# Four pieces of an fp4 weight rounding moved from the front into the layers, and all weight transposes into the last stage

## The reference, cut to what matters

```python
# 1. token part: patches -> 9 windows per token, local attention over them, then one global class token
q = ln(red) @ la_wq;  k, v = ln(win) @ la_wkv;  agg = softmax(q*scale @ k) @ v
local = red + agg @ la_proj_w + la_proj_b
cls_out = cls + attention(ln(cls) @ ga_wq, ln(local) @ ga_wkv) @ ga_proj_w + ga_proj_b
h = concat([local @ mod_w + mod_b, cls_out])
# 2. two layers of delta-rule attention and a gated feed-forward part, on layernorm(h)
h = h + attn(layernorm(h))
# 3. feed-forward part whose activations and weights are rounded to fp4 in blocks of 16
def fp4_quant_dequant(x):
    scale = max(max(abs(xb)) / 6, 1e-12)                  # one per 16 values
    return GRID[searchsorted(MID, abs(xb / scale))] * sign(xb) * scale
h = h + fp4_linear(silu(fp4_linear(y, w_gate)) * fp4_linear(y, w_up), w_down)   # y = layernorm(h)
```

## Time and profile before

| | us |
|---|---|
| median of 3 runs | 394.76 |
| lowest and highest | 392.4, 395.17 |
| profiled execution | 392.98 |
| its span | 391.2 |

### The profile page before, as it was taken

The page is one execution under the profiler, slowest core; times in us unless marked ns, Lnnn a source line. Parts: engine busy times, 40 slices in busy tenths (PEclk is TensorE's granted clock), DMA queues, the critical chain, the costliest instruction groups (busy, mean ns, idle before and its releaser), DMA issues.

```text
span 391.2 us, 9485 instructions
## 1 busy us (share of the span) xinstructions
PE 309.1 (79%) x4346; PEld 228.1 (58%) x4346; DVE 204.0 (52%) x359; ACT 88.7 (23%) x187; POOL 43.9 (11%) x33
## 2 busy tenths in 40 slices
PE   0999449968992478698388999897488999868966
PEld 0556346757981356465387857565487857555443
DVE  3029987995469436214755222114755221159993
ACT  1132002301211013455012122255012122231020
POOL 0744951200032000000000000000000000000000
PEclk9999958998998559899688699999588599989989
DMA  8999910000000000000000030230000000000001
GB/s 187 333 330 215 339 61 0 3 0 0 1 2 0 0 0 2 1 0 2 2 2 3 2 109 2 59 169 2 3 0 3 2 3 0 1 0 0 2 0 34
DMA packets 2521, 18.26 MB, mean 47 GB/s; under 512 B 441, under 2 KB 761, under 8 KB 1729
## 3 DMA queue, kind: packets, MB, share of 16 engines
q1 hardware_dynamic: 2497, 17.91, 15.0%
HBM read 17.58 MB, written 0.33 MB: 46 GB/s over the span
## 4 chain that ended last, share of the span: by engine, by line
PE 47%; DVE 31%; DMA 10%; ACT 5%; issue 3%; POOL 3%; SPq 1%; DVEq 0%; ACTq 0%
DMA big<-in_patches 10%; PE ps L1229 10%; PE ps L1074 5%; PE ps L1225 4%; PE ps L1014 4%; PE ps L1378 3%; PE ps L1293 3%; PE ps L1341 2%; DVE big L891 2%; PE ps L1024 2%; DVE big L919 2%; DVE qa L572 2%; PE ps L1302 2%; DVE wt L916 2%; DVE big L901 2%
## 5 line engine op out<-in xcount | busy, mean ns | idle before, releaser
L1024 PE MATMUL ps<-big,cwb 120*128 120x384 f32 x120 | 42.8, 515 | 10.4 <-DMA big<-in_patches 10.4
L1024 PEld LDWEIGHTS ps<-big,cwb 120*128 120x128 f32 x120 | 24.1, 204 | 26.7 <-issue 13.5
L1074 PE MATMUL ps<-wkvg,pecT 128*128 128x256 f32 x144 | 33.7, 395 | 4.8 <-ACT big L360 4.8
L1225 PE MATMUL ps<-cst,ones 128*128 128x320 f32 x112 | 36.5, 476 | 0.0
L1074 PEld LDWEIGHTS ps<-wkvg,pecT 128*128 128x128 f32 x144 | 28.2, 198 | 9.1 <-DVE prod L687 3.7
L1229 PE MATMUL ps<-cwb,wl 128*128 128x320 f32 x120 | 33.3, 435 | 0.0
L1225 PEld LDWEIGHTS ps<-cst,ones 128*128 128x128 f32 x112 | 23.4, 214 | 9.9 <-issue 2.6
L1229 PEld LDWEIGHTS ps<-cwb,wl 128*128 128x128 f32 x120 | 22.5, 190 | 10.6 <-issue 0.9
L1293 PE MATMUL ps<-wt,big 32*32 32x32 f32 x1280 | 16.6, 213 | 13.0 <-DVE wt L894 10.6
L262 POOL TENSOR_TENSOR xs<-xs,big 120x640 f32<-120x640 f32 x14 | 22.8, 1629 | 8.6 <-DMA big<-in_patches 7.8
L1293 PEld LDWEIGHTS ps<-wt,big 32*32 32x32 f32 x1280 | 14.9, 125 | 15.1 <-DVE wt L894 11.5
(11 more groups left out here) (224 smaller groups left out, 485.8 us busy)
## 6 DMA issues: line engine op xcount, KB each, us to landing
big<-in_patches SPq DMA_DIRECT2D x6, 900.0 KB, 26.2
wl<-in_layers SPq DMA_DIRECT2D x2, 2176.0 KB, 26.8
wt<-in_tok SPq DMA_DIRECT2D x1, 2304.0 KB, 17.7
wf<-in_ffn SPq DMA_DIRECT2D x1, 2112.0 KB, 26.4
wl<-in_layers SPq DMA_DIRECT2D x2, 1040.0 KB, 23.2
cwb<-in_conv SPq DMA_DIRECT2D x1, 600.0 KB, 5.1
out<-h SPq DMA_DIRECT2D x5, 64.0 KB, 2.0
cst<-in_constants SPq DMA_DIRECT2D x1, 304.0 KB, 39.4
```

The lines of the kernel that those rows point to most:

```text
L1024: last = mm(ps[:, i % 4, 0:GRP], cwc[:, k, c * P:(c + 1) * P], xg[:, g, k, :], start=(k == 0), stop=(k == KC - 1))
L1074: last = mm(ps[:, 2 * w + un % 2, t * C:(t + 1) * C], pecT[:, c, i * P:(i + 1) * P], wkvg[:, c, w * C:(w + 1) * C], start=(c == 0), stop=( ...
L1225: mm(ps[:, bank, 0:NT], ones[:, :], cst[:, 0:NT], start=True, stop=True)
```

## The change

Pieces 0 and 1 of the rounding stay in the front. Piece 2 + 2l goes to the head of layer l, behind `normed`; piece 3 + 2l to its end, one part ahead of each addition into x and the last part behind them. All nine groups of transposes go to the last stage, behind the transposes of x, into banks 6 and 7, and all weight copies on ScalarE behind its last table load. The twelve clock-holding products there become four, behind the weight transposes. `sf` moves from `wf` to columns 3200 to 7040 of `big`, and GpSimd's zeroing of a part of `act` waits for the scores of the global attention in place of the last transposes.

```diff
--- before.py
+++ after.py
@@ -132,7 +132,7 @@
         rkq = pf[:, 2560:3840].rearrange("p (a j n) -> p a j n", a=2, j=CH)
         bt = pf[:, 3840:4480].rearrange("p (j n) -> p j n", j=CH)
 
-        sf = wf[:, :]
+        sf = big[:, 3200:7040]
         kh = sf[:, 0:640].rearrange("p (j n) -> p j n", j=CH)
         kbq = sf[:, 640:1920].rearrange("p (a j n) -> p a j n", a=2, j=CH)
         act = sf[:, 1920:3840].rearrange("p (i n) -> p i n", i=FC)
@@ -280,7 +280,7 @@
             w1 = sc[:, 1, :, HD:H].unsqueeze(3).broadcast_to([P, NP_, H - HD, DH])
             nc.gpsimd.tensor_tensor(v1, v1, w1, ALU.mult).then_inc(S["vprod"], 1)
 
-            pool.wait_ge(S["wq_t"], 9)
+            pool.wait_ge(S["ga_s"], 1)
             nc.gpsimd.memset(act[0:64, FC - 1, :], 0.0).then_inc(S["zeros"], 1)
             for l in range(LAYERS):
 
@@ -365,7 +365,7 @@
 
                 for i in range(first, end):
                     act_.wait_ge(S["wq_t"], i + 1)
-                    b = 4 + i % 2
+                    b = 6 + i % 2
                     if i < 6:
                         nt = min(4, 11 * 2 - 4 * i)
                         dst = wguT[:, :, :].rearrange("p c (i n) -> p i c n", i=11)[:, 2 * i:2 * i + nt // 2]
@@ -408,11 +408,9 @@
             rsqrt(act_, rsg, ps[:, 1, 0:NW], "ga_rs", EPS_LN, k=1)
             act_.wait_ge(S["ga_max"], 2)
             nc.scalar.activation(ge[:, :, :, :], ge[:, :, :, :], ACT.Exp, scale=SCALE).then_inc(S["ga_e"], 1)
-            weights_out(0, 6)
 
             act_.wait_ge(S["x_c"], 1)
             nc.scalar.activation(sqx[:, :, :], xT[:, :, :], ACT.Square).then_inc(S["x_sq"], 1)
-            weights_out(6, 9)
             act_.wait_ge(S["x_var"], 1)
             rsqrt(act_, rs[:, :], ps[:, 1, 0:NT], "x_rs", EPS_LN, k=1)
 
@@ -497,6 +495,7 @@
             act_.wait_ge(S["stats"], 6)
             rsqrt(act_, rs3[:, :], mv[:, :, 1], "rs3", EPS_LN, k=1)
             nc.scalar.preload_act_table_set("silu_and_others")
+            weights_out(0, 9)
 
             def x_across(p):
                 n = P if p < 2 else 64
@@ -758,25 +757,14 @@
 
             for part in range(3):
                 weights(1, part)
-            weights(2, 0)
             red_a(0)
-            weights(2, 1)
             red_b(0)
-            weights(2, 2)
-            weights(3, 0)
-            weights(3, 1)
             red_c(0)
-            weights(3, 2)
-            for part in range(3):
-                weights(4, part)
             scores_bias(0)
-            weights(5, 0)
             red_a(1)
             scores(0)
-            weights(5, 1)
             red_b(1)
             scores(1)
-            weights(5, 2)
             scores(2)
             red_c(1)
             for un in range(3, 5):
@@ -868,6 +856,8 @@
 
             def layer(l):
                 normed(l, 0, V_N1)
+                for part in range(3):
+                    weights(2 + 2 * l, part)
 
                 dve.wait_ge(S["silu"], EACH["silu"] * l + 10)
                 v.scalar_tensor_tensor(bv[:, :, :], tb.unsqueeze(2).broadcast_to([P, NG, DH]), 1.0, vs[:, :, :],
@@ -959,8 +949,10 @@
                     b = 3 + i % 3 if i < FC - 1 else i % 3
                     v.tensor_tensor(act[r, i, :], sg[r, i % 2, :], ps[r, b, 0:NT], ALU.mult).then_inc(S["act"], 1)
                 for j in range(CH):
+                    weights(3 + 2 * l, j)
                     dve.wait_ge(S["dn_mm"], EACH["dn_mm"] * l + j + 1)
                     v.tensor_tensor(xT[:, j, :], xT[:, j, :], ps[:, 6 + j, 0:NT], ALU.add).then_inc(S["x"], 1)
+                weights(3 + 2 * l, 2)
 
             for l in range(LAYERS):
                 layer(l)
@@ -1149,7 +1141,9 @@
             def weights_across(first, end):
 
                 for i in range(first, end):
-                    b = 4 + i % 2
+                    b = 6 + i % 2
+                    if i == 0 or i == 6:
+                        pe.wait_ge(S["wq"], 4 if i == 0 else 6)
                     if i >= 2:
                         pe.wait_ge(S["wqT"], i - 1)
                     if i < 6:
@@ -1197,10 +1191,8 @@
                     last = mm(ps[:, 3, j * NW:(j + 1) * NW], gwkv[:, c, C + j * P:C + (j + 1) * P], lga[:, c, :],
                               start=(c == 0), stop=(c == CH - 1))
             last.then_inc(S["ga_gv"], 1)
-            pe.wait_ge(S["wq"], 6)
             pe.wait_ge(S["aggT"], 2)
             pe.wait_ge(S["loc"], 4)
-            weights_across(0, 6)
             pe.wait_ge(S["ga_agg"], 3)
             for j in range(CH):
                 for c in range(CH):
@@ -1209,10 +1201,8 @@
             last.then_inc(S["ga_proj"], 1)
             pe.wait_ge(S["h0"], 4)
             norm_sum(ps[:, 0, 0:NT], hT0[:, :, :], ones[:, :]).then_inc(S["x_mean"], 1)
-            weights_across(6, 9)
             pe.wait_ge(S["x_sq"], 1)
             norm_sum(ps[:, 1, 0:NT], sqx[:, :, :], ones[:, :]).then_inc(S["x_var"], 1)
-            pe.wait_ge(S["wqT"], 10)
             pe.wait_ge(S["x_rs"], 1)
 
             def norm(l, half):
@@ -1391,8 +1381,11 @@
                     o_ = ps[:, 1, C * p + c * P:C * p + (c + 1) * P] if p < 2 else ps[0:64, 2, c * P:(c + 1) * P]
                     last = nc.tensor.transpose(o_, hT0[:, c, P * p:P * p + n], ident)
             last.then_inc(S["h1_t"], 1)
-            keep_clock(6, 12)
+            pe.wait_ge(S["x"], EACH["x"] * LAYERS + 2)
+            weights_across(0, 9)
+            keep_clock(3, 4)
             pe.wait_ge(S["h1"], 2)
+            pe.wait_ge(S["wqT"], 10)
             for p in range(3):
 
                 n = P if p < 2 else 64
```

## The result

The change made the kernel slower: 401.56 us median (401.19 to 401.86, 4 runs) against 393.87 for the kernel before (392.4 to 395.17), a ratio of 1.0196 [1.0152, 1.024]. The forecast was 396.8, with 401.5 as its upper end. The profiled execution took 401.52 us for a span of 399.7, which is 8.5 above that of before.

A forecast was written before the change was run, and what follows sets the result against it. Between the stages the kernel was taken as one chain of waits, with TensorE's clock priced in every term. Front -3.8, global attention +2.9, layers 0 and last stage +3.8 gave +2.9 and a median of 396.8 us, range 391.0 to 401.5.

The forecast's parts named there:

- Front, -3.8: Keys and values: with pieces 2 to 5 gone, unit 3 starts earlier and runs faster; 3.8 us won, bounds -1.9 and -4.2.
- The 1.9 of the shorter pause: Front: VectorE centres at once after the mean, so unit 3 starts near 86.2 in place of 88.17.
- The 1.8 of the clock: Front: after a pause of 1.5 us the clock stays high, so unit 3 takes 3.54 us for 5.38.
- Global attention, +2.9: Global attention: without transposes TensorE's clock is low until layer 0 holds it; 2.9 us lost, bounds -1.1 and +4.9.
- The rival that the clock does not fall: Global attention: the few groups suffice to hold the clock; sum -1.2, some 393 us for the median; chance 0.22.
- the rival that the terms of the clock do not matter: Whole kernel: clock terms cancel or do not matter, the skill's rule; sum +0.5, 393.5 to 395 us; chance 0.10.
- the 1.0 and 1.1 of the forecast: Global attention: at the low clock the variance loses 1.0 us and the first norm 1.1.
- a gain of 0.9 (-1.1 + 0.2): Global attention: last matrix's transposes leave from before the variance sums, -1.1; two small groups before the variance slow, +0.2.
- "Nothing again": Layers: rounding pieces at each layer's end fit into VectorE's pauses, 0.45 to 0.7 us to spare each; cost 0, bound +3.4.
- "rounding in the layers is not hidden": Layers: the moved rounding costs 3.4 us on top, time 399 to 400 us; chance 0.05.
- Last stage, +3.8: Last stage: weight copies, transposes and holding products make TensorE late for x; 3.8 us lost, bounds +2.7 and +6.3.
- The rival of +6.3: Last stage becomes the bound: low clock for transposes and holding products, first tile's gate 6.3 later; 400 to 402; chance 0.16.

The follow-up runs named there:

- the second experiment: The changed kernel with the rounding of pieces 2 to 5 left out altogether: 402.37 us, ratio 1.0261 to the kernel before.
- the first experiment: The changed kernel with 13 clock-holding products on TensorE in the pauses of the global attention: 398.03 us, ratio 1.0108 to the kernel before.
- the ninth experiment: The changed kernel with holding products, padded stream, transposes in the layers, and the last three transpose groups out of x's way: 387.58 us, ratio 0.9858 to the kernel before.

## Why the prediction was wrong

**Front, -3.8: right in the trace, half of it by the phase of the clock.** -3.62, with both halves as worked out (pause 1.58, unit 3 3.69), and 3.7 us on the median when it is undone. The 1.9 of the shorter pause are in every kernel. The 1.8 of the clock are a gain only against executions like the one that I read: in two of the five traces with the rounding in the front, unit 3 took 3.69 after the same pause of 3.52, and the global attention took some 1.5 more in the same traces. I had priced the two stretches as independent.

**Global attention, +2.9: the mechanism right, its parts not all.** The rival that the clock does not fall is refuted by the windows at 0.50, and so is the rival that the terms of the clock do not matter: keeping it up won 3.5 us. The variance lost 1.25 and the norm 1.11, near the 1.0 and 1.1 of the forecast, and the holding products 0.2 to 0.3 in place of 1.5. From the aggregate's product to the variance I had forecast a gain of 0.9 (-1.1 + 0.2), and the trace has a loss of 0.4: the two small groups ran wholly at the low level (1.94 and 2.50 us for 1.10 and 1.94), 1.4 in place of 0.2. Ahead of the aggregate 0.8 were won where I had put a loss of 0.2. That the sum came within 0.7 is partly errors that cancel, in a stretch that differs by 2.3 us between executions.

**Layers, "Nothing again": the step that failed.** +3.18. Two of its three parts stand: the rounding is hidden (its removal wins nothing), and the moved tiles are free. What failed is what I did not count. I priced the 34 transposes as 34 transposes, in the place that they leave and in the place that they come to. They are also 68 instructions between the start and the layers, and their leaving moves everything behind them in TensorE's instruction stream. That this position makes up the whole 3.18 is shown from both sides: 68 put back 171.29 and 171.45, 256 more 171.18, as in the kernel before; 188 more 175.13, with the rounding absent 174.64, and with only 52 of the 68 put back 174.81. The rival "rounding in the layers is not hidden" had nearly this price, +3.4, by another cause, which the second experiment excludes.

How the position becomes time is argued, not shown. The pauses are 1.28, 0.37 and 1.40 in both layers together after the change and 0.88 and 0.72 before, 1.45 us more, but the layers do not follow this sum: it is 0.55 with 68 put back and 1.60 in the kernel before, with the same layers, and 1.59 in the first experiment, whose layers are as long as those of the changed kernel. What the slow kernels have in common is a pause of 0.9 us or more in the first passes of at least one layer's loop (at granted clock 0.50 in the changed kernel), which the others have not. The low level takes about 52 us of the layers in place of 45 (from 0.85 and 0.87), which goes the same way.

The Trainium skill (Runtime: NRT & Kernel Launch, "Instruction fetch mechanics") says that instructions are refilled in blocks of 16 KiB, 256 of them, and that crossing a boundary is mostly hidden. The size agrees with the packets of 16 KB and with the 256 that change nothing, and "mostly" agrees with the ten transfers and two pauses counted above. Where one is not hidden, in a stretch of dense small products, it stopped TensorE for 0.15 to 1.60 us here, and where it falls was worth 3.2 us.

**Last stage, +3.8: right.** +4.26, with the idle time before `hh` at 4.25 where 3 to 4 were expected, and gone in the ninth experiment, when the transposes are placed elsewhere. The rival of +6.3 did not come about.

**The first and the last stretch, 0: +1.17 and +1.32, open.** In the first, VectorE loses rounding from 53.82 on, but in these two traces the difference lies in the products of the fifth group of patches, which wait for nothing and ran at clock 0.72 (8.91 us to the next step) in place of 0.85 (7.60). The stretch is 76.96 to 77.95 long in the five kernels with the rounding in the front and 76.91 to 78.58 in the nine without, so no cost of the change is shown there. In the last stretch the final product takes 4.30 us after the change and 2.94 before, the same twelve halves. Seven of the fourteen kernels have 2.94 and seven 4.30 to 5.56, and the second experiment, with the last stage of the changed kernel, has the short one; what sets it I did not find.

The sum: 8.5 found less 2.9 forecast is 5.6, and that is 3.2 of the layers, 2.5 of the two open stretches, 0.5 of the last stage and 0.2 of the front, less 0.7 of the global attention.

## What to carry to other kernels

Moving work that costs nothing where it stands can cost where it is missing: those transposes filled pauses that would otherwise drop TensorE's clock, so fill such a pause with other work, or leave them. When instructions move from ahead of a dense loop to behind it, the stream's block boundaries shift inside that loop; look for "issue" pauses in the first passes of such a loop behind 16 KB transfers, and try a few instructions more ahead of the loop, since a whole round of 256 changes nothing. And a move is only as good as its landing: nine groups of transposes put in a row before the first step that needs the engine cost 4.3 us, and spread over pauses of engines that wait anyway, with the clock held and the stream put back, they left 1.4% of gain. Last, read a stretch in several executions before pricing its clock: the same pause of 3.52 us had a slow unit behind it in three traces and a fast one in two.

## What the runs showed of the hardware

In the loops of the layers, pauses of TensorE's stream without a releaser, 0.15 to 1.60 us long, come behind some of the 16 KB packets of the instruction queue (two behind ten in the kernel before). Their place moves with the count of instructions ahead of them, and 188 instructions more cost 3.8 us of time where 256 more cost none. The granted clock behind the same pause of 3.5 us was 1.00 in two kernels and 0.76 in three.
